# Recurrent block with a routed feed-forward: who issues the broadcast loads of delta

## What is computed

```python
# branch s: a selective state-space layer, 128 channels, 64 states per channel
y = layernorm(xn) * gamma + beta
left, right = split(y @ W_up + b_up)
left = silu(causal_conv3(left))
delta = softplus(left @ W_delta + b_delta);  Bm = left @ W_B;  Cm = left @ W_C
h[t] = exp(delta[t] * A) * h[t-1] + (delta[t] * left[t]) * Bm[t]     # per channel and state
s = xn + (((h[t] * Cm[t]).sum(states) + left * D) * silu(right)) @ W_down + b_down
# branch f: 8 experts, top 2 per token, hidden size 1024
f = sum over the 2 chosen experts of w_e * (silu(xn @ w1_e) * (xn @ w3_e)) @ w2_e
out = x + s * silu(f)
```

## Time and profile before

| | |
|---|---|
| median of 3 runs | 1404.51 us (1402.75 to 1405.11) |
| the profiled execution | 1398.48 us |
| its span | 1396.4 us |
| TensorE busy | 1242.4 us, 89% |
| VectorE busy | 1191.0 us, 85% |
| GpSimd busy | 1114.0 us, 80% |
| ScalarE busy | 754.3 us, 54% |
| DMA, loads of delta (ScalarE's queue, q10) | 134.25 MB, 32.7% of the 16 engines' time |
| DMA, SyncE's queue (q1) | 61.82 MB, 13.6% |
| DMA, GpSimd's queue (q0) | 20.46 MB, 4.6% |

### The profile page before, as it was taken

How to read it: one execution, slowest core, us unless ns; L and a number is a source line. 1 busy time by engine, 2 the same in 40 slices (tenths; PEclk the granted TensorE clock), 3 DMA queues, 4 the chain that set the end, 5 groups by cost and what they waited for, 6 DMA issues and landing times. The chain is left out here.

```text
span 1396.4 us, 21735 instructions
## 1 busy us (share of the span) xinstructions
PE 1242.4 (89%) x5800; PEld 913.5 (65%) x5800; DVE 1191.0 (85%) x1618; ACT 754.3 (54%) x1613; POOL 1114.0 (80%) x1090
## 2 busy tenths in 40 slices
PE   5847799999999999999999999999999999977730
PEld 5725367777777777777777777777677677754410
DVE  6747579998899889988999889988898899988858
ACT  1351566555655575557555675557555755555521
POOL 0356279898999798888998898989997888898863
PEclk9978999999999999999999999999999999975555
DMA  6111265447555646564574457446545564654346
GB/s 209 61 38 46 68 212 175 143 129 220 147 150 150 188 149 181 161 195 130 170 224 136 122 183 222 133 122 220 171 137 168 172 172 138 198 186 130 115 147 229
DMA packets 124965, 218.04 MB, mean 156 GB/s; under 512 B 15264, under 2 KB 40992, under 8 KB 124832
## 3 DMA queue, kind: packets, MB, share of 16 engines
q10 hardware_dynamic: 73728, 134.25, 32.7%
q1 hardware_dynamic: 43616, 61.82, 13.6%
q0 software_dynamic: 7488, 20.46, 4.6%
HBM read 191.57 MB, written 24.90 MB: 155 GB/s over the span
## 5 line engine op out<-in xcount | busy, mean ns | idle before, releaser
L416 POOL TENSOR_TENSOR arena<-arena,c_rep 128x512 f32<-128x512 f32 x512 | 602.4, 1181 | 129.2 <-DVE arena L954 117.0
L954 DVE TENSOR_TENSOR_SCAN arena<-bank,carry,arena 128x512 f32<-128x512 f32 x512 | 652.6, 1275 | 36.9 <-ACT bank L724 34.9
L1189 PE MATMUL bank<-xgT,wring 128*128 128x256 f32 x2240 | 536.5, 382 | 1.0 <-issue 1.0
L1189 PEld LDWEIGHTS bank<-xgT,wring 128*128 128x128 f32 x2240 | 419.0, 190 | 120.3 <-issue 59.9
L724 ACT ACTIVATE bank<-arena,a_neg 128x512 f32<-128x512 f32 x512 | 354.3, 692 | 94.5 <-DVE arena L954 41.0
L945 DVE TENSOR_TENSOR arena<-bank,b_rep 128x512 f32<-128x512 f32 x512 | 351.7, 687 | 47.7 <-PE bank L1202 31.0
L1202 PE MATMUL bank<-stack,pick 128*128 128x512 f32 x512 | 298.3, 589 | 4.7 <-DVE arena L945 4.5
L648 ACT ACTIVATE th<-bank 128x256 f32<-128x256 f32 x312 | 119.2, 382 | 297.1 <-PE bank L1189 222.8
L1158 PE MATMUL bank<-wring,hid 128*128 128x256 f32 x1120 | 270.6, 384 | 2.3 <-POOL hid L431 2.3
L1158 PEld LDWEIGHTS bank<-wring,hid 128*128 128x128 f32 x1120 | 210.4, 191 | 62.7 <-issue 25.2
L431 POOL TENSOR_TENSOR hid<-gt,ue 128x256 f32<-128x256 f32 x312 | 226.9, 727 | 2.0 <-DVE gt L966 1.9
(11 more groups left out here) (167 smaller groups left out, 847.6 us busy)
## 6 DMA issues: line engine op xcount, KB each, us to landing
arena<-delta_d ACTq DMA_DIRECT2D x512, 256.0 KB
wring<-in_w_all SPq DMA_DIRECT2D x64, 384.0 KB, 5.1
arena<-results SPq DMA_DIRECT2D x16, 512.0 KB, 6.3
xn<-in_x SPq DMA_DIRECT2D x4, 1024.0 KB, 9.5
xn_d<-xn SPq DMA_DIRECT2D x4, 1024.0 KB, 5.3
parts_d<-spare SPq DMA_DIRECT2D x16, 256.0 KB
stack<-parts_d SPq DMA_DIRECT2D x16, 256.0 KB
out<-arena SPq DMA_DIRECT2D x8, 512.0 KB, 3.1
```

Source lines behind the costliest of these rows:

```text
L416: pool.tensor_tensor(p_ring[:, s % P_RING, :], h_ring[:, s % H_RING, :], of_chunk(c_rep, c, 2), ALU.mult).then_inc(s_hc, 1)
L954: v.tensor_tensor_scan(out=h_ring[:, s % H_RING, :], data0=a_bank[s % 2][:, :], data1=b_ring[:, s % B_RING, :], initial=carry[:, q:q + 1], ...
L1189: ins = pe.matmul(bank[:, m * SLOT:(m + 1) * SLOT], wring[:, kk, (2 * m + h) * P:(2 * m + h + 1) * P], xgT[:, i % 2, h, :], start=(h == 0) ...
```

## The change

`load_delta` moves, with its waits, from ScalarE's program to SyncE's. SyncE issues the first three loads once the tables of the routing are there, and at the head of its pair `s` the load for pair `s + 3`, ahead of its own work of that pair. Nothing else is altered: sizes, slots, semaphores and the amount of data are the same.

```diff
@@ SyncE's program
+            def load_delta(s):
+
+                c, ch = s // PAIRS, 32 * (s % 4) + 2 * ((s % PAIRS) // 4)
+                if s % PAIRS == 0:
+                    sp.wait_ge(s_partd, STORES * (c + 1))
+                ge(sp, s_exp, s - D_RING + 1)
+                sp.dma_start(dl_ring[:, s % D_RING, :], delta_d[ch:ch + 2, cols(c)].unsqueeze(0).broadcast_to([N, 2, CH])
+                             ).then_inc(s_dl[s % D_RING], 16)
+
             store_parts(0)
             load_stack(0)
+            sp.wait_ge(s_table, 1)
+            for s in range(D_RING - 1):
+                load_delta(s)
             for s in range(PAIR_COUNT):
                 c, at = s // PAIRS, s % PAIRS
+                if s + D_RING - 1 < PAIR_COUNT:
+                    load_delta(s + D_RING - 1)
                 for name, cc, r in WORK[s]:
@@ ScalarE's program
-            def load_delta(s):
-
-                c, ch = s // PAIRS, 32 * (s % 4) + 2 * ((s % PAIRS) // 4)
-                if s % PAIRS == 0:
-                    act.wait_ge(s_partd, STORES * (c + 1))
-                ge(act, s_exp, s - D_RING + 1)
-                act.dma_start(dl_ring[:, s % D_RING, :], delta_d[ch:ch + 2, cols(c)].unsqueeze(0).broadcast_to([N, 2, CH])
-                              ).then_inc(s_dl[s % D_RING], 16)
...
             act.wait_ge(s_setup, 2)
-            act.wait_ge(s_table, 1)
-            for s in range(D_RING - 1):
-                load_delta(s)
 
             for s in range(PAIR_COUNT):
-                if s + D_RING - 1 < PAIR_COUNT:
-                    load_delta(s + D_RING - 1)
                 act.wait_ge(s_dl[s % D_RING], 16 * (s // D_RING + 1))
```

## The result

| | before | after |
|---|---|---|
| median | 1403.63 us (8 runs, 1399.42 to 1405.14) | 1413.22 us (8 runs, 1410.07 to 1417.54) |
| ratio, 95% interval | | 1.0077 (1.0057 to 1.0098) |
| profiled execution, span | 1396.4 us | 1414.3 us |

The change makes the kernel slower. The medians are 9.6 us apart, 0.7%; the ratio is formed over all the runs and not from the two medians, and says 0.8%, with an interval of 8.0 to 13.8 us.

The account below looks back on a forecast made before the run. TensorE was taken as nearly full (1060.71 of 1077 us), then a chain of short waits at the end. Terms -1.5 + 6.5 + 1 + 0.5 = +6.5 us, on the median 1404.51, gave 1411.0 us, range 1402 to 1418.

Parts of the forecast that it names:

- The reads of x in front of pair 464: SyncE's queue: pair 464's load of delta waits behind eight reads of x, 4.19 MB; +6.5 us (+4 to +9).
- with 2 us won back: After the stop at pair 464, VectorE catches up: 8.7 us late less 2.2 gives +6.5 us.
- rival 3: TensorE's clock falls with the stall near 1223 us, slowing its products there: +4 us, 1415; chance 0.13.
- The traffic jam: At 830 to 850 us, loads of delta queue behind weight loads taking 7.0 us: +1 us (0 to 4).
- the first weights: Pair 17's load of delta stands behind the first eight weight blocks, 3.15 MB: +0.5 us (0 to 2).
- ScalarE's relief: ScalarE loses 512 issues, so exponentials no longer wait behind them: -1.5 us, between nothing and 6 us gained.
- The first exponential: At 115.27 us, it comes 3.9 us after the first issue and will again: no change.
- Weights of a new expert: At 28 places two 384 KB weight blocks precede a load of delta; tightest cover 0.7 us holds: 0.
- The check that I had set: The prediction is wrong if the loop up to pair 460 has moved by over 4 us either way.
- Rival 1: Loads mix with reads even within SyncE's queue; pair 464's usable before 1221 us; 1403.5, down to 1399; chance 0.2.
- Rival 2: SyncE becomes the gate: loads behind two weight blocks stall the tight places, 14 us on top, 1425; chance 0.12.

Follow-up runs that it names:

- e1: Changed kernel, but the eight reads of x issued one per pair at pairs 460 to 467, not all at pair 460: 1404.57 us, ratio 1.0018.
- e2: Changed kernel, but the loads of delta for pairs 464 to 467 issued by ScalarE: 1407.20 us, ratio 1.0035.
- e6: Changed kernel, but the reads of x in two groups of four, at pairs 460 and 464: 1409.21 us, ratio 1.0050.
- e4: e1, plus the first expert's weight blocks two per pair at pairs 13 to 16, later groups' second block one pair later: 1401.19 us, ratio 0.9993.

## Why the prediction was right, and where its terms were off

The forecast was +6.5 us to 1411.0, range 1402 to 1418; measured were 1413.2 and +9.6. Direction, place and mechanism were right. The size was low: every term that was off came out on the slow side of its value. The terms found add up to 11.4 us, against a forecast of 6.5 and a measured distance of 9.6 (8.0 to 13.8). A little of the closeness of the 1411.0 is luck: it stood on a median of 1404.51 us before, from 3 runs, and over 8 runs that was 1403.63. Term by term, with the changed kernel's first and second profile:

- **The reads of x in front of pair 464: +6.5 predicted, +8.3 and +8.3 found.** The working was close up to the stop itself: usable 16.6 us after the first read (15.8 found), scan 8.7 us late (8.0 found: it starts 16.55 us after the first read in place of 8.57), TensorE's stop 5.5 us (5.51). It counted from the start of the reads, and so came out right without saying that SyncE itself would reach the load only after 7.2 us. What failed is the step "with 2 us won back" (the sum took off 2.2). VectorE won back 0.7 us at pair 465, and 1.3 us were lost again at pair 468. Those are rival 3 in a small size: eight products of an expert's step took TensorE 3.38 us there in place of 1.89 us, in the window with the granted clock of 0.66, and ScalarE waited for them:

```profile
1240.90 3.38 PE L1189 MATMUL bank<-xgT,wring 128*128 128x256 f32 x8
...
1244.32 0.38 ACT L653 ACTIVATE th<-bank 128x256 f32<-128x256 f32 x1 [4.64 <-PE bank L1189]
```

  Its full size (+4) did not come.
- **The traffic jam: +1 predicted, +1.9 and +2.6 found; the first weights: +0.5, and +1.4 and +0.8 found.** Both within their ranges. The reading under the first was off: the late loads between 830 and 851 us made up 5.1 of the 11.1 us before, not most of them. At pair 17 the changed kernel's exponential waits 2.3 us for the load behind eight weight blocks:

```profile
183.20 5.56 SPq L327 DMA_DIRECT2D wring<-in_w_all  x8
...
189.01 12.44 SPq L340 DMA_DIRECT2D arena<-delta_d  x8
...
196.01 0.69 ACT L724 ACTIVATE bank<-arena,a_neg 128x512 f32<-128x512 f32 x1 [2.30 <-DMA arena<-delta_d]
```

- **ScalarE's relief: -1.5 predicted, about -0.4 found over 273 pairs.** The prediction expected the scans' waits for exponentials to fall to some 25 us outside the one stall; they were 49.1 - 7.9 = 41.2 us. The failed step is taking the exponential's wait for itself as exposed: behind it stood the waits for the scan two pairs back and for TensorE's products, which took over. That TensorE, at 1060.71 of 1077 us, would have passed on little of any gain is argued, not shown.
- **The first exponential: 0 predicted, 2.8 us late found.** The prediction took the 3.9 us from issue to exponential as fixed. They are now 5.2 us (118.03 - 112.85), since the table's load no longer runs beside the DMA. What it cost the whole is open, as said above.
- **Weights of a new expert: 0 predicted, 0 found** outside the jam. The staircase is flat over the other groups, and loads came late 10 times in all.
- **The check that I had set, that the loop up to pair 460 moves by under 4 us, failed as read**: it had moved by 9.4 and 9.1 us in the two profiles, and by 5.7 to 8.0 us in e1, e2 and e6. In the first profile some 3 us of it are the steps of the change and 6.2 us the first column and the step at pair 420, where the clock fell. I had not thought of what the clock can move before pair 17, nor of the late start. By this sign the prediction called itself wrong, though its main term was right.

Rival 1 (the queue does not matter) is refuted by the packets of the changed kernel and by e2: with the reads in flight, loads in ScalarE's queue are on time and one in SyncE's is not. The time alone would not have told: with the 7.2 us that the eight issues really took, in place of the rival's 3.3, and the 7.5 us of before from issue to use, the rival comes to 14.7 us from the first read, against 15.8 found. The sentence of the Trainium skill's page DMA: Bandwidth & Descriptors, section Issuing engines are not separate DMA queues, that transfers run on the same 16 engines and interleave whichever engine issued them, holds between two queues, as the earlier trace rows show. It speaks of different issuers and not of two transfers from one, so the prediction made more of it than it says; its second half, that another issuer saves only issue time, does not fit here, where four loads put back to ScalarE made the kernel 6.0 us faster. The section Queues, rings and completion order of that page (one ring in order, turns between queues) agrees with both the packets within q1 and the sharing of q1 and q10. Rival 2 (SyncE as the gate) did not show: e4 keeps all of SyncE's waits at the outs and costs nothing that can be measured.

Left open: why the clock's steps before pair 15 and at pair 420 come in some executions and not in others. Whether the change makes the one at pair 420 likelier, and what the late start costs, is open too.

## What to carry to other kernels

A small load with a deadline belongs in a queue in which nothing large is put in front of it. When a transfer is moved to another engine's queue, list everything that queue issues, and compare the engine time of the largest burst plus the load's own (here 12.4 + 3.9 us) with the time from the start of the burst to the use (here 6.7 us). A burst of 6.2 us looks short enough beside the 6.7 us alone, and still made its load 3.5 us late. If the load must share, deal out the burst one piece per step. That an engine's issue costs 0.5 us each says nothing about what removing it gains: look at what the freed instruction waits for next. And look at what ran beside the loads at the start, here the load of a table, and whether it still does.

## What the runs showed of the hardware

- Within SyncE's queue the data moved in the order of issue: in the 6 us after the load of delta was issued, all of the queue's 1919 packets were smaller than the load's data packets of 2 KB, and the load's first such packet started 6.9 us after its issue, at the end of the eight reads.
- With eight reads of 512 KB in a row the issue of one went from 0.41 us to 1.42 us in the changed kernel, and up to 3.30 us in the kernel before, where ScalarE's loads shared the engines:

```profile
1215.58 3.30 SPq L356 DMA_DIRECT2D b_rep<-in_x  x1
```

- A load of delta from ScalarE takes 0.52 us to issue, one of half the size 0.61 us in the median of 1024: the issue's time does not go with the bytes.
- The load of ScalarE's table for the exponential (1.28 us) came ahead of the wait for the DMA where ScalarE itself had issued DMAs just before, and behind that wait where it had not.
- TensorE's granted clock falls to the lower of its two levels for 3 to 7 us at a time in some executions of the same program and not in others (e1, e2 and e6 against the changed kernel, up to pair 15). Two such falls cost 4.7 us; the distance at pair 15 between these profiles is 2 to 3 us.
